# Cross-attention stage: x1, x2 and the probabilities turned in 32x32 blocks on DVE and carried by DMA

## What is computed

```python
x = _layernorm(x + _L0_attn_ref(x, ...))             # mixer; the result is called x1 below
x = _layernorm(x + _L0_xattn_ref(x, ctx_1024, ...))  # cross attention; the result is x2
x = _layernorm(x + _L0_ffn_ref(x, ...))              # slots, experts, combine

# _L0_xattn_ref, 16 heads of 32
q = (x @ q_w + q_b); k = (context @ k_w + k_b); v = (context @ v_w + v_b)
att = jnp.einsum('bhtd,bhsd->bhts', q, k) / jnp.sqrt(jnp.float32(D))
att = jax.nn.softmax(jnp.where(causal, att, -jnp.inf), axis=-1)
y = jnp.einsum('bhts,bhsd->bhtd', att, v) @ o_w + o_b
# the first step of _L0_ffn_ref: 16 slots x 16 heads = 256 rows attend over all 2048 tokens x2
```

## Time and profile before

| | us |
|---|---|
| median of 3 runs | 1525.36 |
| lowest and highest | 1524.46, 1530.15 |
| span of the profiled execution | 1522.9 |
| PE busy | 1380.7 (91%) |
| DVE busy | 801.1 (53%) |
| ACT busy | 445.1 (29%) |
| POOL busy | 216.9 (14%) |
| moved by DMA | 309.31 MB |

### The profile page before, as it was taken

The page is one execution under the profiler, slowest core; times in us unless marked ns, Lnnn a source line. Parts: engine busy times, 40 slices in busy tenths (PEclk is TensorE's granted clock), DMA queues, the critical chain, the costliest instruction groups (busy, mean ns, idle before and its releaser), DMA issues.

```text
span 1522.9 us, 26477 instructions
## 1 busy us (share of the span) xinstructions
PE 1380.7 (91%) x10061; PEld 863.6 (57%) x10061; DVE 801.1 (53%) x2171; ACT 445.1 (29%) x935; POOL 216.9 (14%) x181
## 2 busy tenths in 40 slices
PE   8899999999999999999999999876767776679997
PEld 5777777777667777777777776221111111127664
DVE  1666676776787767777677774000000000004998
ACT  2434434334244444444444442000000000002333
POOL 1111121021031212212122121000000000001221
PEclk9999999999999999999999999997787888789999
DMA  9443133132212241144111137999999999995663
GB/s 353 139 152 97 56 98 97 43 97 84 84 36 84 98 168 48 49 166 154 56 48 48 55 138 272 414 418 425 427 427 426 424 428 426 424 423 189 205 233 114
DMA packets 75004, 309.31 MB, mean 203 GB/s; under 512 B 8923, under 2 KB 14171, under 8 KB 57000
## 3 DMA queue, kind: packets, MB, share of 16 engines
q1 hardware_dynamic: 72616, 293.49, 50.2%
q10 hardware_dynamic: 2304, 14.68, 2.7%
HBM read 274.33 MB, written 33.82 MB: 202 GB/s over the span
## 4 chain that ended last, share of the span: by engine, by line
PE 51%; DMA 21%; DVE 16%; issue 4%; ACT 3%; POOL 0%; DVEq 0%; ACTq 0%; POOLq 0%
DMA all_ring<-in_e_Wg 21%; PE mxw_bank L994 7%; PE mxw_bank L1043 6%; PE mxw_bank L178 5%; PE mix_scores L1712 4%; PE mxw_bank L1084 4%; PE mxw_bank L1104 3%; PE mix_scores L1014 3%; DVE all_ring L248 3%; PE mix_scores L1007 2%; PE mxw_bank L1023 2%; PE mix_scores L791 2%; PE mix_scores L1735 2%; PE mxw_bank L1067 1%; PE mix_scores L761 1%
## 5 line engine op out<-in xcount | busy, mean ns | idle before, releaser
L1712 PE MATMUL mix_scores<-all_ring,all_space 128*32 128x512 f32 x968 | 152.1, 729 | 77.7 <-DMA all_ring<-in_e_W 39.4
L1762 DVE TENSOR_TENSOR all_space<-all_space 128x512 f32<-128x512 f32 x16 | 11.1, 694 | 376.6 <-ACT all_space L1771 376.6
L178 PE MATMUL mxw_bank<-all_ring,all_space 128*128 128x256 f32 x768 | 180.3, 389 | 1.6 <-DMA all_space<-in_WinT 1.6
L178 PEld LDWEIGHTS mxw_bank<-all_ring,all_space 128*128 128x128 f32 x768 | 145.6, 193 | 33.4 <-issue 10.8
L1771 ACT ACTIVATE all_space<-mix_scores 128x512 f32<-128x512 f32 x32 | 19.1, 597 | 404.5 <-PE mix_scores L1721 404.5
L1712 PEld LDWEIGHTS mix_scores<-all_ring,all_space 128*32 128x32 f32 x968 | 31.5, 121 | 182.4 <-DMA all_ring<-in_e_Wg 67.9
L1269 POOL TENSOR_TENSOR all_space<-all_space 128x1232 f32<-128x1232 f32 x32 | 72.2, 2256 | 393.9 <-DVE all_space L1217 393.9
L994 PE MATMUL mxw_bank<-all_space 128*128 128x128 f32 x1024 | 119.8, 275 | 0.0
L1735 PE MATMUL mix_scores<-all_ring,all_space 128*32 128x512 f32 x480 | 108.6, 709 | 10.2 <-DVE all_space L1765 10.2
L994 PEld LDWEIGHTS mxw_bank<-all_space 128*128 128x128 f32 x1024 | 116.9, 192 | 0.7 <-issue 0.5
L248 DVE SCALAR_TENSOR_TENSOR all_ring<-all_ring,all_space 128x256 f32<-128x256 f32 x192 | 84.5, 482 | 53.4 <-ACT all_ring L197 50.9
(11 more groups left out here) (319 smaller groups left out, 2204.8 us busy)
## 6 DMA issues: line engine op xcount, KB each, us to landing
all_ring<-in_e_W SPq DMA_DIRECT2D x55, 2048.0 KB, 24.7
all_ring<-in_e_Wg SPq DMA_DIRECT2D x28, 2048.0 KB, 26.2
all_ring<-in_xT SPq DMA_DIRECT2D x8, 1024.0 KB, 8.6
all_ring<-scratch_rates SPq DMA_DIRECT2D x64, 128.0 KB, 4.1
all_z<-in_x SPq DMA_DIRECT2D x16, 512.0 KB, 4.0
all_space<-scratch_x SPq DMA_DIRECT2D x32, 256.0 KB, 2.8
scratch_x<-all_space SPq DMA_DIRECT2D x32, 256.0 KB, 2.0
scratch_x2T<-all_space SPq DMA_DIRECT2D x32, 256.0 KB, 2.0
```

The source lines that it names most:

```text
L178: last = nc.tensor.matmul(bank[:, i * BT:(i + 1) * BT], hold["win"][:, k, m * P:(m + 1) * P], hold["xT"][b % 2][:, k, :], start=(k == 0), ...
L1712: last = nc.tensor.matmul(bank[w][q * ROWS:(q + 1) * ROWS, :], hm[u][:, k, :], weights[k % 2][:, q * FQ:(q + 1) * FQ], start=(k == 0), sto ...
```

## The change

x1 and x2 are no longer turned by PE, nor are the probabilities. DVE turns them in 32x32 blocks, which leaves the blocks themselves in the wrong place, and DMAs carry the blocks to where they belong:

- x1: in the mixer, `turn_rows` turns a chunk on DVE (128x1024), and `store` writes the blocks to a new DRAM tensor x1T with eight more DMAs (`store_blocks`, 128 rows of 512 bytes each). `load_x1T` reads a tile of it.
- probabilities: `turn_probs` on DVE turns 16 heads x 96 columns (77 and padding), 1536 elements, and `move_probs` on SP copies the blocks from SBUF to SBUF in twelve DMAs.
- x2: `turn_x2` on DVE, four `store_blocks` DMAs to x2T, and one `load_x2T` back. The last tile is still turned by PE.
- The features are now ordered in quads, so three weight matrices come permuted, and the combine stage's score is done in four times as many matmuls with 32 stationary columns.

Besides, `take_queries` moves from DVE to ACT; the LayerNorm root is Exp(-0.5 Ln(var + eps)) on ACT (`norm_factors`), with one table set that holds both, loaded at the start; and the work of a tile is spread over more steps: a step has scores of t+2, queries of t+3, values and output of t, and the slot parts of t-2. PE waits in `weigh_values` for twelve DMAs (`prT_in`) in place of ACT's copies.

```diff
+                nc.scalar.preload_act_table_set("natural_log_exp_and_others")
...
+def store_blocks(eng, to, t, blocks, stored):
+
+    for i in range(QUADS):
+        eng.dma_start(to[bass.ds(t * P, P), i * P:(i + 1) * P].rearrange("(j f) n -> f j n", j=QUADS),
+                      blocks[i * QUAD:(i + 1) * QUAD, :].rearrange("f (j n) -> f j n", j=QUADS)).then_inc(stored, 16)
...
+        sp.wait_ge(s["x1_turned"], c + 1)
+        for b in range(BATCH):
+            store_blocks(sp, io["x1T"], b * CHUNKS + c, x1blk[:, b, :], s["x1T_stored"])
...
+    def turn_rows(dve, c):
+
+        dve.wait_ge(s["x1_done"], c + 1)
+        wait_later(dve, s["x1T_stored"], 16 * QUADS * BATCH * c)
+        nc.vector.transpose(x1blk[:].rearrange("p b d -> p (b d)"), x1[c % 2][:].rearrange("p b d -> p (b d)")).then_inc(s["x1_turned"], 1)
...
+    def load_x2T(sp, t, u):
+
+        if isinstance(t, int):
+            wait_later(sp, s["slot_sc"], t - 1)
+        sp.wait_ge(s["x2T_stored"], X2T_BLOCKS * (t + 1))
+        sp.dma_start(x2T[u][:].rearrange("p i k t -> p (i k t)"), io["x2T"][bass.ds(t * P, P), :]).then_inc(x2T_in[u], 16)
...
+    def move_probs(sp, t):
+
+        sp.wait_ge(s["pT_done"], t + 1)
+        wait_later(sp, s["av_done"], t)
+        for j in range(SBLOCKS):
+            n = min(QUAD, CTX - j * QUAD)
+            for i in range(QUADS):
+                sp.dma_start(prT[j * QUAD:j * QUAD + n, i, :, :], pT[i * QUAD:i * QUAD + n, j, :, :]).then_inc(s["prT_in"], 16)
...
+    def weigh_values(pe, t, b):
+        ahead_by = 4 if known(t, *range(OTHER)) else 3
+        pe.wait_ge(s["qT_done"], min(t + ahead_by, TILES) if isinstance(t, int) else t + ahead_by)
+        pe.wait_ge(s["prT_in"], PROBS_IN * (t + 1))
...
+    def take_queries(act, t):
+        act.wait_ge(s["q_done"], t + 1)
+        wait_later(act, s["sc_done"], t)
+        for g in range(GROUPS):
+            last = nc.scalar.activation(qT[:, g, :], AV[:, g * P:(g + 1) * P], ACT.Identity, bias=qbias[:, g:g + 1])
+        last.then_inc(s["qT_done"], 1)
...
+    def norm_factors(act, t):
+
+        act.wait_ge(s["agg_done"], t + 1)
+        nc.scalar.activation(minus_mean, mean, ACT.Copy, scale=-1.0)
+        nc.scalar.activation(log_var, var, ACT.Ln, bias=eps).then_inc(s["ln_act"], 1)
+        act.wait_ge(s["ln_act"], 3 * t + 1)
+        nc.scalar.activation(rstd, log_var, ACT.Exp, scale=-0.5).then_inc(s["ln_act"], 1)
+        act.wait_ge(s["ln_act"], 3 * t + 2)
+        nc.scalar.activation(shift_by, minus_mean, ACT.Copy, scale=rstd).then_inc(s["ln_act"], 1)
...
+    def turn_probs(dve, t):
+
+        dve.wait_ge(s["normed"], t + 1)
+        wait_later(dve, s["prT_in"], PROBS_IN * t)
+        nc.vector.transpose(pT[:], pr[:].rearrange("p h (j f) -> p j h f", f=QUAD)).then_inc(s["pT_done"], 1)
+
+    def turn_x2(dve, t, u):
+        dve.wait_ge(s["x2_done"], t + 1)
+        wait_later(dve, s["x2T_stored"], X2T_BLOCKS * t)
+        nc.vector.transpose(x2blk[:], x2[u][:]).then_inc(s["x2_turned"], 1)
...
+                if ahead(t, 4):
+                    load_x1T(sp, t + 4, u)
...
+                    store_x2T(sp, t - 1)
+                if ahead(t, 1):
+                    move_probs(sp, t + 1)
+                if before(t, 1):
+                    load_x2T(sp, t - 1, 1 - u)
...
-                turn_probs(pe, t)
...
                 weigh_values(pe, t, seq(0))
-                if before(t, 1):
-                    turn_x2(pe, t - 1, 1 - u)
-                if at_end(t):
-                    slots["turn_token"](pe, 0, 0)
-                    project_out(pe, t)
-                    slot_scores(pe, t - 1, 1 - u)
-                    return
-                if ahead(t, 1):
-                    score(pe, t + 1, seq(1))
-                if before(t, 1):
-                    slot_scores(pe, t - 1, 1 - u)
+                if before(t, 2):
+                    slot_scores(pe, t - 2, u, half - 1)
+                if ahead(t, 3) and not known(t, *range(OTHER)):
+                    score(pe, t + 2, seq(2))
+                    queries(pe, t + 3, 1 - u, half + 1 + u)
+                if before(t, 2):
+                    turn_slots(pe, t - 2)
                 project_out(pe, t)
-                if before(t, 1):
-                    turn_slots(pe, t - 1)
-                if ahead(t, 2):
-                    queries(pe, t + 2)
-                if before(t, 1):
-                    weigh_tokens(pe, t - 1, 1 - u)
+                if before(t, 2):
+                    weigh_tokens(pe, t - 2, u)
...
+                if before(t, 1):
+                    norm_factors(act, t - 1)
...
+                if c >= 2:
+                    first["turn_rows"](dve, c - 2)
...
+                if before(t, 3):
+                    add_tokens(dve, t - 3, 1 - u, seq(-3))
+                if ahead(t, 1):
+                    turn_probs(dve, t + 1)
+                if before(t, 1) and not known(t, LAST - 2):
+                    turn_x2(dve, t - 1, 1 - u)
+                if known(t, LAST - 2):
+                    take_scores(dve, t + 2, False)
+                    turn_x2(dve, t - 1, 1 - u)
                 if before(t, 2):
-                    add_tokens(dve, t - 2, seq(-2))
-                if ahead(t, 1) and before(t, 1):
-                    take_queries(dve, t + 1)
-                if isinstance(t, int) and t == 1:
-                    first["norm"](dve, END)
-                if isinstance(t, int) and t == LAST - 1:
+                    slot_maxima(dve, t - 2, seq(-2))
+                if ahead(t, 2) and not known(t, LAST - 2):
+                    take_scores(dve, t + 2, known(t, CHUNKS - 2))
+                if before(t, 2):
+                    slot_sums(dve, t - 2, u, seq(-2))
+                if ahead(t, 2):
+                    denominators(dve, t + 2)
+                if known(t, LAST - 1):
                     slots["invert_sums"](dve, 0)
                     for m in range(SM):
                         slots["divide_tokens"](dve, 0, m)
-                if at_end(t):
-                    norm_last(dve, u)
+                if known(t, LAST):
...
-                last = nc.tensor.matmul(SCORES[u][:, j * SROWS:(j + 1) * SROWS], x2T[u][:, j, k, :], hold["m2"][:, b, k, :],
-                                        start=(k == 0), stop=(k == KC - 1))
+                for q in range(QUADS):
+                    last = nc.tensor.matmul(SCORES[u][q * QUAD:(q + 1) * QUAD, j * SROWS:(j + 1) * SROWS], x2T[u][:, j, q, k, :], hold["m2"][:, b, k, :],
+                                            start=(k == 0), stop=(k == KC - 1))

```

More of the change, by code:

```diff
@@ L944, in cross_rows @@
     d = Place(space, hold["tiles_at"], SPACE - 238 - GROUPS)
-    x2T = [d.sb([P, KC, P]) for i in range(2)]
+    x2T = [d.sb([P, QUADS, KC, QUAD]) for i in range(2)]
     x2 = [d.sb([P, D]) for i in range(2)]
@@ L1315, in _ @@
                     sp.dma_start(hold["qbias"][:], io["q_b"]).then_inc(hold["cross_in"], 16)
[L1316 to L1322 removed]
+            load_x1T(sp, 2, 0)
```

530 lines of the change are left out of this document (271 added, 259 removed).

## The result

The changed kernel takes 1606.20 us (median of four runs, 1605.01 to 1607.49), the kernel before, beside it, 1525.88 us. The ratio is 1.0517, with a 95% interval of 1.05 to 1.0534. Forecast were 1480 us and a range up to 1520. The profiled execution has a span of 1605.4 us against 1522.9, 82.5 more.

| piece, measured between starts on TensorE | before | after | change | forecast |
|---|---|---|---|---|
| up to the first `project_out` | 427.71 | 456.29 | +28.6 | +19.7 |
| its first five tiles | 80.4 | 91.2 | +10.8 | -3 |
| tiles 5 to 30 (25 tiles) | 395.8 | 422.7 | +26.9 | -64.3 |
| from tile 30 to the experts' first matmul | 42.3 | 53.8 | +11.5 | 0 |
| from there to the end | 576.7 | 581.5 | +4.8 | +2 |

The account below looks back on a forecast made before the run. TensorE was taken as the bound, cross-stage tiles going from 15.83 to 13.2 us: 64.3 us gained, less 2 at start, 14.7 in the mixer and 2 in combine, from 1522.9 plus 2.5 to 1480 us; range 1462 to 1520.

Parts of the forecast that it names:

- chain over SP and the DMA: Cross stage: project_out through DVE, SP's stores and twelve copies to weigh_values, once in two tiles, allowing 13.05 us a tile.
- TensorE's loss of three groups: Cross stage: the transposes of the probabilities, x1 and x2 leave TensorE, together 2.86 us of a 15.77 us tile.
- floor: Cross stage: TensorE's remaining groups take 12.91 us a tile if nobody makes TensorE wait.
- DVE: Cross stage: work kept 9.19 us, two transposes 2.45, open wait for ACT's Exp 1.06; 12.7 us a tile.
- Rival (a): DVE's transposes in cross stage and mixer cost twice the price per element, 14.8 us a tile, 1542 us; chance 0.07.
- the sign named for it: Cross stage: TensorE waiting at weigh_values for the probabilities' copies by more than 0.5 us a tile means SP's chain is longer.
- rival (b): Cross stage: SP's chain is longer, 13.95 us a tile, 1498 us, chance 0.18; dear end 15.7, 1542 us, chance 0.05.
- The first five tiles: Start of the cross stage: 80.4 us before, 77 with DVE's work and SP's waits, a gain of 3 us.
- The mixer: Before the cross stage: DVE's turn of x1 adds 1.22 us to each of 12 chunks, 14.7 us lost.
- The start: Ahead of the first project_out: two more query blocks on TensorE against the turns leaving, 5 us later.
- The tail: End of the cross stage: one more slot_scores (1.89 us) against Newton gone (2.8 against four short ACT steps), even.
- The combine stage: Score in 32 narrow matmuls in place of 8: at worst 7 us, 2 us taken as lost.

Follow-up runs that it names:

- e9: e8 with the probabilities' store issued ahead of x2's four block stores, and the mixer's turn ahead of the taps as in e1: 1519.44 us.
- e10: e9 with the experts' first weights loaded as twelve 1 MB halves in twelve tiles, not six 2 MB loads in six: 1517.25 us.
- e12: e10 with SP issuing the small loads of the experts' rows and biases ahead of the load of tile 30's x2: 1512.72 us.
- e13: e12 with the first load of x1's turned rows issued one mixer chunk earlier: 1503.30 us, ratio 0.9866 to the kernel before.
- e4: The changed kernel with six of the twelve probabilities' copies issued from ACT's queue: 1548.28 us.
- e8: The changed kernel with the probabilities' blocks carried through device memory, one store and three loads for twelve copies; turn_probs waits for the store only: 1566.97 us.
- e2: The changed kernel with a second buffer for the probabilities' turned blocks, so turn_probs waits for the copies one tile further back: 1587.20 us.
- e5: The changed kernel with the six 2 MB loads of the experts' first weights issued behind the cross stage: 1598.33 us, one run.
- e1: The changed kernel with DVE's turn of x1's rows in the mixer moved ahead of the taps: 1595.23 us.

## Why the prediction was wrong

The direction was wrong, and the time lies beyond every rival, of which the slowest ended at 1545. What the prediction took as the bound of the kernel before was right, and so was most of what it priced; the step that failed is its chain over SP and the DMA, 26.1 us for two tiles, in which one issue of the probabilities' copies was taken as 0.40 us and is 0.69.

- **TensorE's loss of three groups: right, its floor 0.3 us too low.** The quiet tiles of e9, e10, e12 and e13 take 13.2 to 13.4 us, so the stage gets to the forecast once the transport is short enough. But in a tile of 13.2 TensorE does not wait at all: that is the floor itself, since slot_scores, queries and weigh_tokens each take 0.1 us longer than in the earlier trace rows. The forecast had 12.91 and 0.3 for engines that do not mesh; that the sum fits is luck.
- **DVE: right.** `turn_probs` takes 1.77 us and turn_x2 0.67, for 1.76 and 0.69. Rival (a), the slow transpose, is out. The wait for ACT's Exp is 1.05 us, for 1.06. With 11.1 us of work a tile DVE is below the 11.64 forecast, and even in e9's quiet tiles it is busy for 83%, not over 90.
- **SP and the DMA: the failing step.** The chain of two tiles was counted as 26.1 us and is 30.7, and the sign named for it came: `weigh_values` waits 2 us in every second tile, where 0.5 a tile was the mark. Of the 4.6, the copies' issues are +3.5 (12 x 0.69 for 12 x 0.40), the clock behind the wait +1.55, a wait of 0.55 for x2T's load and some 0.4 of small ones on TensorE +1.0, DVE's part -0.5, the landing -1.0. I had taken the price of an issue near the plain form; the dear end, 0.65, was the nearer one, and even it is below the measured 0.69. e4 shows it by moving half of the copies to another queue and changing nothing else; e8 and e9 agree, with other edits beside.
- **A ring left out.** The text followed the copies to `weigh_values(t+2)` only. `turn_probs` also waits for the landing of the tile before, in one tile. With my own numbers that ring is 1.76 + 0.69 + 2.0 + 4.8 + 2.4 = 11.7 us and does not bind; with the crowded tile's it is 19.5 and does. It was in the diff, in the wait of `turn_probs`, and should have been priced at the dear ends like the rest: 1.76 + 0.69 + 2.6 + 7.8 + 4.1 = 17.0. e2 opens it and gains 19 us.
- **The landing beside big loads.** The row with 4.1 us was the dear end of the range; in the crowded tiles it is 7. I named the 2 MB loads on ACT's queue as a reason for rival (b) and gave them no price. e5 puts them at 1.2 us a tile.
- **The clock** stood nowhere in the sum. Before, TensorE had no wait in the 78 us of the earlier trace rows. After, a wait of 2 us is paid with 1.55 us more in the next group, or with 4.4 in the next three.
- **The first five tiles**, +10.8 for -3: tiles 1 to 4 take 14 to 23 us with the mixer's last rows, the block stores and 1 MB loads in them. e13 still has 88.1 us there for 77 forecast. Which of these is how much was not separated.
- **The mixer: right.** 12 x 1.22 = 14.7 us were forecast; by the fifteenth chunk the scores come 13.5 us later, 1.16 a chunk, and the turn takes 1.24 us. That it need not be paid (e1) could be read in the earlier trace rows, from DVE's 3.07 us of waiting.
- **The start**, 5 us for some 15: the first load of x1's turned rows was queued on SP behind the stores and TensorE stood 6.4 us for it, then 1.8 for the clock; e13 gets 7.5 back at the first `project_out`. I had counted TensorE's groups there and not the load.
- **The tail**, 0 for 11.5: in e10's chain the block stores of x2 of tile 30 land 11.5 us after their issue beside 2 MB loads, SP stands behind them at load_x2T, and the small loads of the experts behind SP; as changed TensorE waits 5.58 us at the same place for the same loads (L1981 <- POOL). e12 gets 8.7 us of it back on TensorE, between tile 30 and the experts.
- **The combine stage: right.** From the experts' last matmuls to the end 152.5 us for 151.1, +1.4 where 2 were taken. The other 3.4 us behind the stage are in the expert stage; in e10 they are not there.

Rival (b) had the mechanism, with 0.18 and 0.05. Its dear end, 1542, fell short since it took the range of an issue and a landing from quiet rows and counted one chain. The rule of the Trainium skill that 128x128 blocks belong on TensorE ("VectorE: DVE Perf Modes", section "Rules for kernel authors"), which I quoted against the change, gave 1525 and no gain; the change as made is worse than that. With the other transport and e1's, e10's, e12's and e13's edits the move gains 1.3%; the kernel before was not run with such edits of its own. The rule of the Trainium skill on small transfers ("DMA: Bandwidth & Descriptors", section "Measured (HBM→SBUF, 128 partitions, SWDGE, issued from GpSimd)"), to which I gave no chance, pointed at the right place for another reason: not each transfer's fixed time one after another, but 0.69 us of issue for each copy on one queue.

## What to carry to other kernels

Work that moves from a full engine to an idle one brings its transport with it: count DMA issues on the queue that makes them like instructions on an engine, at the dearest form in sight, and walk every wait of the new steps around until it meets itself, over one tile and over two. Do not take a small transfer for a cheap issue: 13 rows cost more than 32 here. Price a landing once alone and once beside the largest load that shares the engines. Short of an idle queue, make fewer and larger transfers, and put one's landing under another's issues; a step that has slack goes where its engine waits already. Left open: no run moves x1 and x2 only and keeps the probabilities, whose copies are the failing piece, on TensorE; none pads the 13 rows.
